# Two transformer layers on one core: bias and mask matmuls as pairs of 64-row tiles

## The chip, the cores and the metric

One core of a Trainium2 chip. The metric is the device time of one execution in microseconds (us). The kernel before took 1443.73 us (median of 3 runs, 1442.54 to 1447.4).

## What is computed

The input is 2 sequences of 1024 tokens with 128 channels. Two layers follow each other, each of the form x + attention(norm(x)) * silu(ffn(norm(x))). Only attention matters here:

```python
# layer 0: 16 heads of 8 channels, 2 x 1024 tokens, additive position bias, no mask
energy = jnp.einsum('bhqd,bhkd->bhqk', q, k)
rel = jnp.clip(pos[:, None] - pos[None, :] + (N - 1), 0, bias_table.shape[0] - 1)   # 249 rows
energy = energy + bias_table[rel].transpose(2, 0, 1)[None]
att = jax.nn.softmax(energy / (scaling * temp), axis=-1)
out = jnp.einsum('bhqk,bhkd->bhqd', att, v)
# layer 1: 16 heads of 8 channels, one sequence per batch, causal
attn = jnp.where(causal, jnp.einsum('bhqd,bhkd->bhqk', Q, K) * scale, -inf)
y = jnp.einsum('bhqk,bhkd->bhqd', jax.nn.softmax(attn, axis=-1), V)
```

The feed-forward parts are experts: ten in layer 0, a soft routed attention and eight experts in layer 1. As `rel` is clipped to 249 rows and N - 1 is 1023, the bias differs from a constant only where the key stands more than 775 positions after the query: queries of the first two tiles of 128, keys of the last two. The kernel subtracts the constant, which softmax does not see.

## The kernel before

Attention (`attention(l)` in each engine's block) works on groups G of four heads (j = 0 to 3), 8 groups in all, and on two halves of 512 queries in each: 16 halves H. Queries and keys are split in three bf16 parts and stacked on 48 rows (51 in the transposed form, where the maxima come in as three more rows). Heads j = 0 and 2 lie on partitions from 0, j = 1 and 3 on partitions from 64, so that their matmuls stand in different row halves of the array.

Each half has two kinds of scores:
- `s_unit`, 128 queries x up to 512 keys, in four PSUM banks used in turn (`RING`). DVE takes the row maximum of each (L1086), which frees the bank (`ring_free`). From the maxima POOL makes three bf16 parts (L670 to L673), PE turns them (unit "M"), and a DMA puts them as rows into the stack of queries.
- `st_step`, the transposed scores, 128 keys x up to 512 queries, with the maximum already subtracted, in three banks. ACT takes the exponential (L783), and `av_step` multiplies it with the values, four heads in four column tiles of 32.

Where the bias is not constant, or the causal diagonal lies, further matmuls add it into the same bank. In `s_unit` of layer 0, for key half 1 and query tiles 0 (256 columns) and 1 (128 columns), these are three full-array matmuls, one per bf16 part of the bias, with a flipped identity as weights. In `st_step` they are three for key tile 6 and six for key tile 7, with the bias tile `Hst` as weights and the flipped identity as moving operand. The bias tile is Toeplitz: DMAs read it from a DRAM row with a step of one element per partition (`load_bias`, L471). In layer 1, `mask` adds the causal mask as two matmuls of 64 rows in the head's own row half, each with 128 columns:

```python
for n, (w_, m_) in enumerate(zip(weights, moving)):
    ins = mm(out_, w_[row:row + 64, :], m_[row:row + 64, :], start=False, stop=n == 1)
```

`identb_sw` and `mask_kq_sw` are the same tables with their halves of 64 rows exchanged.

The order of PE's work is written out: `s_plan` deals the score units of the coming half over the steps of the present one, and the main loop issues, for each head j of a step, `st_step`, after j = 2 the `av_step` of the step before, and then the units dealt to it. All matmuls go through the helper `mm` (L1303). SP's queue carries all DMAs in program order: before layer 0 the split queries and keys, the bias rows (L531), the gate weights (L533, L541), and in the attention the stacks, bias tiles, maxima rows and the sums' way through DRAM.

The program gives each matmul a division of the array, as rows x columns of a tile: 64x128 for the scores, the transposed scores and the masks, 128x128 for the flips, 128x32 for the values, 128x64 for unit "M".

## Time and profile before

| | |
|---|---|
| median of 3 runs | 1443.73 us |
| profiled execution | 1445.76 us |
| its span | 1443.9 us |
| mean granted clock of TensorE | 0.845 of full speed |
| PE busy | 1172.7 us (81%) |
| DVE, ACT, POOL busy | 925.2, 699.2, 198.6 us |

Layer 0's attention runs from about 250 to 678 us, its transposed scores from 296 us; layer 1's from about 751 to 1121 us, its transposed scores from 810 us. In the rows, `PS<-arena 48*128 48x512` is a score matmul (weights of 48 rows by 128 columns, moving operand 48x512), `51*128` a transposed one, `128*32` a value matmul. The moving operand is named first: `PS<-flip,arena` is a bias matmul of the transposed scores, `PS<-arena,flip` one of the scores, `PS<-mask_kq,identb` a mask matmul of the transposed scores, `PS<-identb,mask_kq` one of the scores. A row of the timeline holds successive instructions with the same names; its length runs from the first start to the last end, and a matmul's end lies some 0.17 us behind its last column, so the distance of starts tells the pace. f32 matmuls appear as two records.

### The profile page before, as it was taken

What the parts mean: (1) busy time and instruction counts of PE and PEld (TensorE: products, weight loads), DVE (VectorE), ACT (ScalarE), POOL (GpSimd) and SP (SyncE); (2) the same over time, 40 slices, a digit from 0 to 9 for tenths busy, and PEclk for the clock granted to TensorE, in tenths of its full rate; (3) what the DMA queues carried; (4) which work ended last, traced back from release to release, by engine and by line L of the source; (5) the groups of instructions that cost most, each with busy time, mean ns of one, the idle gap of its engine ahead of it and who ended that gap; (6) DMA issues with size and microseconds to landing.
All of it is one profiled execution on the core that took longest, in us unless ns stands there. A gap on an engine that the chain in (4) does not pass through costs nothing.

```text
span 1443.9 us, 19168 instructions
## 1 busy us (share of the span) xinstructions
PE 1172.7 (81%) x6931; PEld 555.0 (38%) x6931; DVE 925.2 (64%) x1669; ACT 699.2 (48%) x1326; POOL 198.6 (14%) x292
## 2 busy tenths in 40 slices
PE   5599999779999999989741599889887597887477
PEld 3466666122232222221420244333331274464255
DVE  6687776859888988850651466666661145644577
ACT  5345444057777777774420166655664122121456
POOL 2155553000101100000000001111100300000200
PEclk9799999569999999995955588888885698898778
DMA  5512231501110011000455000000001500000050
GB/s 153 186 41 81 80 99 31 124 11 32 38 34 27 26 31 39 9 17 9 129 138 156 27 10 18 17 18 17 17 18 49 209 1 0 0 0 0 0 235 29
DMA packets 60995, 77.90 MB, mean 54 GB/s; under 512 B 15616, under 2 KB 39792, under 8 KB 57840
## 3 DMA queue, kind: packets, MB, share of 16 engines
q1 hardware_dynamic: 60912, 76.81, 17.2%
q8 instruction: 50, 0.82, 0.2%
q14 instruction: 33, 0.27, 0.1%
HBM read 61.58 MB, written 14.56 MB: 53 GB/s over the span
## 4 chain that ended last, share of the span: by engine, by line
PE 57%; DVE 17%; issue 7%; DMA 6%; ACT 6%; SPq 6%; POOL 1%; DVEq 0%; ACTq 0%; POOLq 0%
PE PS L1303 55%; DVE mx L1086 4%; SPq L464 3%; ACT arena L783 3%; DVE g_hi_lo L1176 3%; DMA arena<-sum_dram 2%; DMA arena<-mrow 2%; ACT g_hi_lo L834 1%; SPq L482 1%; DVE w_hi_lo L1279 1%; PE PS L1316 1%; SPq L449 1%; DVE arena L1288 1%; DMA k_dram<-arena 1%; DVE fw L1189 1%
## 5 line engine op out<-in xcount | busy, mean ns | idle before, releaser
L1303 PE MATMUL PS<-arena 128*32 128x512 f32 (+12 forms) x3680 | 665.1, 517 | 107.8 <-DMA arena<-mrow 78.8
L1086 DVE TENSOR_REDUCE mx<-PS 128x1 f32<-128x512 f32 (+3 forms) x896 | 509.6, 626 | 192.2 <-PE PS L1303 189.0
L783 ACT ACTIVATE arena<-PS 128x512 f32<-128x512 f32 (+3 forms) x896 | 440.9, 555 | 340.2 <-PE PS L1303 336.5
L1303 PEld LDWEIGHTS PS<-arena 128*32 128x32 f32 (+3 forms) x3680 | 168.4, 108 | 503.8 <-DVE mx L1086 138.9
L1176 DVE TENSOR_TENSOR g_hi_lo<-fw,g_hi_lo 128x512 fp32r<-128x512 f32 x80 | 91.7, 1147 | 48.2 <-ACT g_hi_lo L834 48.0
L1303 PE MATMUL PS<-x_hi,w_hi_lo 128*128 128x512 f32 x320 | 113.8, 398 | 0.9 <-DVE fw L1189 0.6
L712 POOL TENSOR_TENSOR fw<-fw,arena 128x512 f32<-128x512 f32 x64 | 90.8, 1423 | 101.0 <-DVE fw L1189 101.0
L842 ACT ACTIVATE fw<-PS 128x512 f32<-128x512 f32 x80 | 47.9, 599 | 97.8 <-PE PS L1303 97.8
L1303 PE MATMUL PS<-g_hi_lo,w_hi_lo 128*128 128x512 f32 x240 | 75.5, 424 | 15.7 <-DVE g_hi_lo L1176 15.7
L1303 PE MATMUL PS<-e_hi_lo,w_hi_lo 128*128 128x512 f32 x192 | 61.8, 404 | 11.7 <-DVE e_hi_lo L1232 11.7
L1303 PEld LDWEIGHTS PS<-x_hi,w_hi_lo 128*128 128x128 f32 x320 | 61.1, 191 | 17.7 <-issue 1.1
L1303 PE MATMUL PS<-x_lo,w_hi_lo 128*128 128x512 f32 x160 | 63.7, 398 | 0.0
L1303 PE MATMUL PS<-identb_sw,mask_kq_sw 64*128 64x128 bf16 x256 | 58.9, 244 | 0.0
L1303 PEld LDWEIGHTS PS<-g_hi_lo,w_hi_lo 128*128 128x128 f32 x240 | 39.7, 188 | 46.9 <-DVE g_hi_lo L1176 42.0
L1303 PE MATMUL PS<-identb,mask_kq 64*128 64x128 bf16 x256 | 57.5, 244 | 0.0
L1189 DVE TENSOR_TENSOR fw<-PS,fw 128x512 f32<-128x512 f32 x80 | 54.4, 680 | 4.7 <-ACT fw L842 4.7
L679 POOL TENSOR_TENSOR arena<-arena 128x512 f32<-128x512 f32 x16 | 20.3, 1271 | 262.4 <-DMA arena<-sum_dram 262.4
L1303 PE MATMUL PS<-mask_kq_sw,identb_sw 64*128 64x128 bf16 x256 | 52.9, 224 | 0.0
L1303 PE MATMUL PS<-mask_kq,identb 64*128 64x128 bf16 x256 | 52.5, 224 | 0.0
L1303 PE MATMUL PS<-e_hi_lo,fw_lo 128*128 128x512 f32 (+1 forms) x128 | 52.1, 407 | 0.0
L670 POOL CAST mparts<-mneg 128x16 bf16<-128x16 f32 x24 | 4.7, 198 | 340.0 <-DVE mneg L1079 340.0
L1316 PE MATMUL PS<-ident,arena 128*128 128x128 f32 x96 | 22.3, 405 | 35.6 <-DVE arena L974 27.9
(219 smaller groups left out, 1208.8 us busy)
## 6 DMA issues: line engine op xcount, KB each, us to landing
arena<-comb_dram SPq DMA_DIRECT2D x24, 1024.0 KB, 7.7
arena<-k_dram SPq DMA_DIRECT2D x16, 408.0 KB
q_dram<-arena SPq DMA_DIRECT2D x24, 256.0 KB, 3.7
k_dram<-arena SPq DMA_DIRECT2D x24, 256.0 KB, 3.8
arena<-q_dram SPq DMA_DIRECT2D x16, 384.0 KB
arena<-drev_dram SPq DMA_DIRECT2D x32, 192.0 KB, 3.6
fw<-sum_dram SPq DMA_DIRECT2D x16, 256.0 KB
arena<-sum_dram SPq DMA_DIRECT2D x16, 256.0 KB
```

The costliest lines, as they stand in the source:

```text
L449: sp.dma_start(dst, src).then_inc(qk_stored[l][b], 16)
L464: sp.dma_start(dst, src).then_inc(att[l][f"ld{n}"], 16)
L482: sp.dma_start(dst, mrow[first:first + 12, H % 2, :]).then_inc(A["m_ld"], 16)
L679: g.tensor_tensor(OT[:, G, 512 * h:512 * (h + 1)], Osb[:, h, :], RB[l][:, h, :], ALU.mult).then_inc(A["r_done"], 1)
L712: g.tensor_tensor(g_, g_, cwb[:, slot, 512 * (u // 2):512 * (u // 2 + 1)], ALU.mult).then_inc(gw_made, 1)
L783: s.activation(Pr[:, m % 8, 0:w], bank(4 + m % 3, 0, w), ACT.Exp).then_inc(A["e_done"], 1)
L842: s.activation(fa[:, u % 2, :], bank(2 * (u % 2)), ACT.Silu).then_inc(a_made, 1)
L1086: v.reduce_max(mx[:, H % 2, kh, n:n + 1], bank(U % RING, 0, w), axis=AX.X, negate=True).then_inc(A["ring_free"], 1)
L1176: v.tensor_tensor(g_r[1][:, u % 4, :], fg[:, u % 4, :], g_r[0][:, u % 4, :], ALU.subtract).then_inc(glo_made, 1)
L1189: v.tensor_tensor(fg[:, u % 4, :], bank(2 * (u % 2) + 1), fa[:, u % 2, :], ALU.mult).then_inc(g_made, 1)
L1303: return nc.tensor.matmul(out_, lhsT, rhs, start=start, stop=stop)
L1316: ins = nc.tensor.transpose(bank(first + c, P * k, P * (k + 1)), src(4 * c + k), ident[:, :])
```

## The change

The full-array bias matmuls are replaced by pairs of 64-row matmuls in the row half of the head, as the masks are, and each of these covers only 64 of the 128 queries. The bias tile in SBUF now holds, for each head, 64 partitions with both halves' values (`Hst[row:row+64, parity, pair, PARTS * half + part, :]`), which needs a second copy of the bias rows in DRAM, shifted by 64 (12 stores instead of 6), and `flip_sw`, the flipped identity with exchanged halves. Two helpers write the matmuls. `add_columns` (the bias of `st_step`, the masks of `s_unit`) restricts the moving operand to 64 columns. `add_rows` (the bias of `s_unit`, the masks of `st_step`) restricts the weights to 64 columns, so that the output has 64 partitions, except for the closing matmul of the bank, which has all 128. A matmul with 64 weight columns gets the division 64x64, one with 128 the division 64x128.

```diff
-        drev_dram = dram("drev_dram", (GROUPS, HG, PARTS, DREV), BF16)
+        drev_dram = dram("drev_dram", (GROUPS, HG, 2, PARTS, DREV), BF16)
...
-        Hst = bf(132, 12).rearrange("p (s j a c) -> p s j a c", s=2, j=HG, a=PARTS)
+        Hst = bf(132, 12).rearrange("p (s r x c) -> p s r x c", s=2, r=PAIRS, x=2 * PARTS)
...
                 for j in range(HG):
-                    src = bass.AP(tensor=drev_dram.tensor, offset=G * (HG * PARTS * DREV) + j * PARTS * DREV,
-                                  ap=[[1, P], [DREV, PARTS], [1, 256]])
-                    sp.dma_start(Hst[:, parity, j, :, :], src).then_inc(h_ld[parity], 16)
+                    row = 64 * (j % 2)
+                    src = bass.AP(tensor=drev_dram.tensor, offset=(G * HG + j) * 2 * PARTS * DREV,
+                                  ap=[[1, 64], [DREV, 2 * PARTS], [1, 256]])
+                    sp.dma_start(Hst[row:row + 64, parity, j // 2, :, :], src).then_inc(h_ld[parity], 16)
...
                 for b in range(BATCH):
-                    dst = drev_dram[b * NG:(b + 1) * NG, :, part, :].rearrange("g j n -> (g j) n")
-                    sp.dma_start(dst, dpart[:, part, :]).then_inc(drev_stored, 16)
+                    for half in range(2):
+                        dst = drev_dram[b * NG:(b + 1) * NG, :, half, part, 0:DREV - 64 * half].rearrange("g j n -> (g j) n")
+                        sp.dma_start(dst, dpart[:, part, 64 * half:DREV]).then_inc(drev_stored, 16)
...
+                    (flip_sw, [[1, P]], -(P // 2 - 1), 1, ALU.not_equal, 1.0),
...
+                    (flip_sw[:, :], [[1, P]], -(P + P // 2 - 1), 1, ALU.not_equal, 1.0),
...
-                def mask(out_, row, weights, moving):
-
-                    for n, (w_, m_) in enumerate(zip(weights, moving)):
-                        ins = mm(out_, w_[row:row + 64, :], m_[row:row + 64, :], start=False, stop=n == 1)
+                def half_rows(row, natural, swapped):
+
+                    return [(natural, swapped)[(half + row // 64) % 2][row:row + 64, :] for half in range(2)]
+
+                def add_rows(out_, permutation, first, moving, last):
+
+
+                    for half in range(2):
+                        ends = last and half == 1
+                        rows = slice(0, P) if ends else slice(first[half], first[half] + 64)
+                        ins = mm(out_[rows], permutation[half][:, rows], moving[half], start=False, stop=ends)
                     return ins
+
+                def add_columns(out_, weights, permutation, first, last):
+
+                    for half in range(2):
+                        c0 = first[half]
+                        ins = mm(out_[:, c0:c0 + 64], weights[half], permutation[half][:, c0:c0 + 64], start=False, stop=last and half == 1)
+                    return ins
+
+                FLIPPED, STRAIGHT = (64, 0), (0, 64)
...
                         for part in range(PARTS):
-                            ins = mm(bank(U % RING, h0, 512), flip[:, :], Hst[:, G % 2, j, part, 0:512 - h0], start=False, stop=part == PARTS - 1)
+                            rows = [Hst[row:row + 64, G % 2, pr, PARTS * half + part, 0:512 - h0] for half in range(2)]
+                            ins = add_rows(bank(U % RING, h0, 512), half_rows(row, flip, flip_sw), FLIPPED, rows, part == PARTS - 1)
                     if masked:
-                        order = (identb, identb_sw) if row == 0 else (identb_sw, identb)
-                        masks = (mask_kq, mask_kq_sw) if row == 0 else (mask_kq_sw, mask_kq)
-                        ins = mask(bank(U % RING, w - P, w), row, masks, order)
+                        ins = add_columns(bank(U % RING, w - P, w), half_rows(row, mask_kq, mask_kq_sw),
+                                          half_rows(row, identb, identb_sw), STRAIGHT, True)
...
-                    for n, (c0, lhsT) in enumerate(extra):
-                        ins = mm(bank(b_, c0, c0 + P), lhsT, flip[:, :], start=False, stop=n == len(extra) - 1)
+                    for n, (c0, part, x0) in enumerate(extra):
+                        weights = [Hst[row:row + 64, G % 2, pr, PARTS * half + part, x0:x0 + P] for half in range(2)]
+                        ins = add_columns(bank(b_, c0, c0 + P), weights, half_rows(row, flip, flip_sw), FLIPPED, n == len(extra) - 1)
                     if masked:
-                        order = (identb, identb_sw) if row == 0 else (identb_sw, identb)
-                        masks = (mask_kq, mask_kq_sw) if row == 0 else (mask_kq_sw, mask_kq)
-                        ins = mask(bank(b_, 0, P), row, order, masks)
+                        ins = add_rows(bank(b_, 0, P), half_rows(row, identb, identb_sw), STRAIGHT,
+                                       half_rows(row, mask_kq, mask_kq_sw), True)
```

The order of PE's instructions at three places. A row names output and inputs (the moving operand first) and the shape of the output, partitions x columns, and the semaphores it waits for. First, the transposed scores of key tile 6 in layer 0, before:

```order
L1303 MATMUL PS<-arena 128x512 [waits e_done0]
L1303 MATMUL PS<-flip,arena 128x128 x3
L1303 MATMUL PS<-arena 128x512 [waits ring_free0]
```

and now:

```order
L1308 MATMUL PS<-arena 128x512 [waits e_done0]
L1308 MATMUL PS<-flip,arena 128x64
L1308 MATMUL PS<-flip_sw,arena 128x64
L1308 MATMUL PS<-flip,arena 128x64
L1308 MATMUL PS<-flip_sw,arena 128x64
L1308 MATMUL PS<-flip,arena 128x64
L1308 MATMUL PS<-flip_sw,arena 128x64
L1308 MATMUL PS<-arena 128x512 [waits ring_free0]
```

Each matmul of 128 columns has become two of 64, all on 128 partitions. Second, the scores of query tile 0 in layer 0, before:

```order
L1303 MATMUL PS<-arena 128x512 [waits ring_free0,h_ld0]
L1303 MATMUL PS<-arena,flip 128x256 x3
L1303 MATMUL PS<-arena 128x512 [waits e_done0]
```

and now:

```order
L1308 MATMUL PS<-arena 128x512 [waits ring_free0,h_ld0]
L1308 MATMUL PS<-arena,flip 64x256
L1308 MATMUL PS<-arena,flip_sw 64x256
L1308 MATMUL PS<-arena,flip 64x256
L1308 MATMUL PS<-arena,flip_sw 64x256
L1308 MATMUL PS<-arena,flip 64x256
L1308 MATMUL PS<-arena,flip_sw 128x256
L1308 MATMUL PS<-arena 128x512 [waits e_done0]
```

Five write 64 partitions, the closing one 128. Third, masked scores and transposed scores in layer 1, before:

```order
L1303 MATMUL PS<-arena 128x384 [waits ring_free1]
L1303 MATMUL PS<-identb_sw,mask_kq_sw 128x128
L1303 MATMUL PS<-identb,mask_kq 128x128
L1303 MATMUL PS<-arena 128x384 [waits e_done1]
L1303 MATMUL PS<-mask_kq,identb 128x128
L1303 MATMUL PS<-mask_kq_sw,identb_sw 128x128
L1303 MATMUL PS<-arena 32x512 [waits e_done1]
```

and now:

```order
L1308 MATMUL PS<-arena 128x384 [waits ring_free1]
L1308 MATMUL PS<-identb_sw,mask_kq_sw 128x64
L1308 MATMUL PS<-identb,mask_kq 128x64
L1308 MATMUL PS<-arena 128x384 [waits e_done1]
L1308 MATMUL PS<-mask_kq,identb 64x128
L1308 MATMUL PS<-mask_kq_sw,identb_sw 128x128
L1308 MATMUL PS<-arena 32x512 [waits e_done1]
```

The scores' masks have half the columns, the transposed scores' first mask half the partitions, and the waits stand where they stood.

## Rows read from the trace of the kernel before

**Rows 1.** The page's chain of work that ended last, by line.
```profile
PE PS L1303 55%; DVE mx L1086 4%; SPq L464 3%; ACT arena L783 3%; DVE g_hi_lo L1176 3%; DMA arena<-sum_dram 2%; DMA arena<-mrow 2%; ACT g_hi_lo L834 1%; SPq L482 1%; DVE w_hi_lo L1279 1%; PE PS L1316 1%; SPq L449 1%; DVE arena L1288 1%; DMA k_dram<-arena 1%; DVE fw L1189 1%
```
**Rows 2.** Stretches: us; PE, PEld, DVE, ACT, POOL busy; clock, DMA share, GB/s.
```profile
296.00:635.00 339.00, 330.63 (x2300) 94.06 (x2296) 292.16 (x501) 256.03 (x485) 30.69 (x75) 0.98 0.10 26
405.64:428.56 22.92, 22.92 (x173) 7.52 (x173) 18.39 (x31) 15.65 (x30) 2.08 (x5) 1.00 0.17 48
810.00:1110.00 300.00, 264.62 (x2448) 113.72 (x2448) 190.70 (x423) 171.28 (x390) 33.40 (x81) 0.80 0.05 16
948.90:976.10 27.20, 26.38 (x283) 12.36 (x283) 20.28 (x43) 17.77 (x42) 2.45 (x6) 0.92 0.05 12
```
**Rows 3.** PE's instructions by form, 948.9 to 976.1 us: busy us, mean ns, idle before.
```profile
L1303 PE MATMUL PS<-mask_kq_sw,identb_sw 64*128 64x128 bf16 x32 | 6.4, 215 | 0.0
...
L1303 PE MATMUL PS<-identb_sw,mask_kq_sw 64*128 64x128 bf16 x28 | 5.7, 219 | 0.0
```
**Rows 4.** Timeline of PE, layer 0: start us, length us, instruction, count.
```profile
408.24 0.34 PE L1303 MATMUL PS<-flip,arena 128*128 128x128 bf16 x3
408.51 0.39 PE L1303 MATMUL PS<-arena 48*128 48x512 bf16 x2
408.83 0.34 PE L1303 MATMUL PS<-flip,arena 128*128 128x128 bf16 x3
409.11 1.39 PE L1303 MATMUL PS<-arena 128*32 128x512 f32 x10
...
411.46 0.39 PE L1303 MATMUL PS<-arena 48*128 48x512 bf16 x2
...
412.23 0.39 PE L1303 MATMUL PS<-arena 48*128 48x512 bf16 x2
```
**Rows 5.** Timeline of PE between the layers; the granted clock there is 0.50.
```profile
740.40 1.96 PE L1303 MATMUL PS<-n1T,router 128*32 128x512 f32 x8 [2.90 <-ACT arena L879]
742.08 1.99 PE L1303 MATMUL PS<-arena,sum_col 128*32 128x512 f32 x8
744.00 0.60 PE L1303 MATMUL PS<-simsq,ones 128*128 128x8 f32 x2
```
**Rows 6.** Timeline of PE in layer 1's routed attention.
```profile
1210.28 0.22 PE L1303 MATMUL PS<-mask_qk,identb 128*128 128x128 bf16 x1
1210.33 0.50 PE L1581 MATMUL PS<-ident,arena 128*128 128x128 f32 x3
```
**Rows 7.** Timeline of PE, layer 1 attention, masks.
```profile
858.76 0.22 PE L1303 MATMUL PS<-mask_kq,identb 64*128 64x128 bf16 x1
858.82 0.21 PE L1303 MATMUL PS<-mask_kq_sw,identb_sw 64*128 64x128 bf16 x1
...
863.03 0.22 PE L1303 MATMUL PS<-identb,mask_kq 64*128 64x128 bf16 x1
...
863.87 0.21 PE L1303 MATMUL PS<-identb_sw,mask_kq_sw 64*128 64x128 bf16 x1
```
**Rows 8.** Groups of instructions, one group of heads of layer 0, 405.64 to 451.47 us.
```profile
L1086 DVE TENSOR_REDUCE mx<-PS 128x1 f32<-128x512 f32 x65 | 40.7, 683 | 5.1 <-PE PS L1303 4.7
```
**Rows 9.** Timeline of PE, layer 0, scores with bias.
```profile
418.54 0.39 PE L1303 MATMUL PS<-arena 48*128 48x512 bf16 x1
...
419.30 0.39 PE L1303 MATMUL PS<-arena 51*128 51x512 bf16 x2
...
424.79 0.39 PE L1303 MATMUL PS<-arena 51*128 51x512 bf16 x2
...
425.38 0.39 PE L1303 MATMUL PS<-arena 51*128 51x512 bf16 x2
```
**Rows 10.** Who waited for whom, 948.9 to 976.1 us: us, times, longest.
```profile
PEld PS L1303 <- DVE mx L1086: 6.8, 10, 1.7
...
PEld PS L1303 <- ACT arena L783: 3.3, 9, 0.6
```
**Rows 11.** Timeline of SP's queue before layer 0's experts.
```profile
44.70 3.43 SPq L531 DMA_DIRECT2D drev_dram<-arena  x6
```

More of the change, by code:

```diff
@@ L202, in block_net @@
         flip = sb("flip", [P, P], BF16)
+        flip_sw = sb("flip_sw", [P, P], BF16)
         identb_sw = sb("identb_sw", [P, P], BF16)
@@ L562, in _ @@
             load_stacks(0, 2)
-            sp.wait_ge(drev_stored, 16 * PARTS * BATCH)
+            sp.wait_ge(drev_stored, 16 * PARTS * BATCH * 2)
             sp.wait_ge(y_done, 8 * FFN_SEQ)
@@ L623, in _ @@
             g.memset(sum_col[:, EXP:EXP + 1], 1.0)
-            for t_ in (ident, identb, flip, mask_kq, mask_qk, identb_sw, mask_kq_sw):
+            for t_ in (ident, identb, flip, flip_sw, mask_kq, mask_qk, identb_sw, mask_kq_sw):
                 g.memset(t_[:, :], 0.0)
@@ L1191, in ffn_units @@
                         weights_lo(n + 1, 1 - slot)
-            dve.wait_ge(drev_stored, 16 * PARTS * BATCH)
+            dve.wait_ge(drev_stored, 16 * PARTS * BATCH * 2)
             ffn_experts(dve, ffn_units)
@@ L1424, in st_step @@
                     if l == 0 and h == 0 and kt == KT - 2:
-                        extra = [(0, Hst[:, G % 2, j, part, 0:P]) for part in range(PARTS)]
+                        extra = [(0, part, 0) for part in range(PARTS)]
                     if l == 0 and h == 0 and kt == KT - 1:
-                        extra = [(q * P, Hst[:, G % 2, j, part, P * (1 - q):P * (2 - q)]) for q in range(2) for part in range(PARTS)]
+                        extra = [(q * P, part, P * (1 - q)) for q in range(2) for part in range(PARTS)]
                     masked = l == 1 and kt * P == q0
```

## The prediction

> **What bounds the kernel now.** I read the page's chain first, then the busy time by stage, then the forms of TensorE's instructions, and last its timeline around the matmuls that the diff touches. The chain lies on PE for 57% of the span, and 55% is line L1303, the matmul helper [rows 1]. By stage [rows 2]: in layer 0's attention (296 to 635 us) PE is busy 330.6 of 339 us at a clock of 0.98, in layer 1's (810 to 1110 us) 264.6 of 300 at 0.80. A group of four heads takes 45.8 us in layer 0. Its first half, which holds the bias matmuls, keeps PE busy throughout (22.92 us; DVE 18.4), so there every nanosecond of PE counts. In layer 1 a group takes some 36.5 us. In 27.2 of them, from 948.9 us, PE is busy 26.4 us at a clock of 0.92, and in the rest the sums go through DRAM and PE waits. The masks stand nearly all in the 27.2 us: the transposed scores' in two forms of 32 matmuls, the scores' in two of 28, one of each shown [rows 3]. So PE's time counts in layer 0's first halves and in layer 1's 27 us.
>
> **What a change of the array's division costs.** Every matmul names a tile of the array, and the timeline shows what it costs to pass from one division to another. Layer 0 [rows 4]: a pair of 512-column matmuls in the two row halves starts at 408.51 us, the full-array flips at 408.83. 512 columns at 2.4 GHz are 0.213 us, so 0.105 us are lost. Three flips cover 0.34 us and one 0.22, so they stand 0.06 us apart (56 ns is what such rows give on longer runs, and 128 columns at 2.4 GHz are 53), but the next matmul comes 0.27 us after the first flip, not 0.17: another 0.095 us. **The rows also show a change of columns alone**: flips on 128x128, then values on 128x32, all with 128 rows, 408.83 to 409.11: 0.28 us, the same 0.1 us too much. At 1.2 GHz the same [rows 5]: eight matmuls on 128x32 take 1.68 us before the next eight start (740.40 to 742.08), and the 128x128 matmul after these comes 1.92 us on, 0.2 too late. It isn't the type: after 128 columns of bf16 an f32 matmul on the same division starts 0.05 us on, 1210.28 to 1210.33 [rows 6]. So I take 0.1 us for each change of division at 2.4 GHz, rows or columns.
> The Trainium skill, TensorEngine Tiling (Array Packing), Tiling Modes, says that changing the mode, not just the tile, drains the engine. It gives no price. It lists 64x64 and 64x128 as two modes, and for that pair no row here shows the price.
>
> **Layer 0, transposed scores (st_step).** 288 full-array flips (by the loops of st_step: 32 places with 3 and 32 with 6) become 576 of 64 columns in the head's own 64 rows with all 128 output partitions: the division of the scores themselves. Both changes of division go. A place with 3 takes 0.59 us now (408.24 to 408.83), one with 6 0.77 (411.46 to 412.23). After: 0.213 us plus 6 or 12 short matmuls. Their spacing s isn't in the trace: 64 columns at 2.4 GHz are 27 ns, the lower end; 56 ns, the flips' own spacing, is the upper, if the weight load or the issue binds. The densest stretch of layer 1 starts 22 matmuls from 863.03 to 863.87, 40 ns apart with their weights and with longer matmuls among them [rows 7]: I take 38 ns. Then 0.44 and 0.67 us, 32 x (0.15 + 0.10) = 8.0 us less; but 16 of the places stand before a value step, whose own change stays: 16 x 0.095 = 1.5 less. **Minus 6.5 us** (27 ns: minus 12.8; 56 ns: plus 3.9). DVE leaves room for it: 40.7 us of reductions in 45.8 [rows 8].
>
> **Layer 0, scores (s_unit).** 192 flips on the full array become 384: of each six, five make 64 partitions (division 64x64) and the last all 128. Two changes before, two after. Today 0.76 us with 256 columns (418.54 to 419.30) and 0.59 with 128 (424.79 to 425.38) [rows 9]. After: 0.213, 0.105, then three rounds if the two column halves of one row half run side by side, as the four value matmuls on 128x32 do, 0.095, and the last matmul, which the next one in the other row half may cover. 256 columns: 0.213 + 0.105 + 3 x 0.107 + 0.095 = 0.73 to 0.84; 128: 0.57 to 0.62. With the middles 32 x 0.025 + 32 x 0.01, **plus 1 us**; at most plus 10 if the halves do not run side by side (32 x 0.32 more).
>
> **Layer 1, transposed scores: the largest term.** 256 masked scores are closed by two mask matmuls of 128 columns, both on 64x128. The two start 0.06 us apart, 858.76 and 858.82 [rows 7]. After, the first mask makes 64 partitions on 64x64, the second all 128 on 64x128. Columns and matmuls stay the same, and two changes of division come in, which were not there: 0.105 + 0.095 = **0.2 us** each. A drain also stops the other row half, which today streams meanwhile (up to 0.1 more), and at 1.2 GHz it costs some 0.2 instead of 0.1 [rows 5]. In a group's 27.2 us stand 32 such scores: 6.4 us. What absorbs it: in these 27.2 us the weight loader waits 6.8 us for DVE's reductions and 3.3 for ACT's exponentials [rows 10], but PE idles only 0.8 us, as most of these waits lie under streaming matmuls. I let 1.5 us be absorbed (0.8 to 5).
>
> **Layer 1, scores.** 512 masks of 128 columns become 512 of 64 columns on the same division, 56 ns to s: 28 units x 2 x 18 ns = 1.0 us per group (0 to 1.6). Together 6.4 - 1.5 - 1.0 = 3.9 us a group, eight groups, **plus 31 us** (0 to 70).
>
> **Small parts.** Bias tiles: the same four issues a group, half the partitions and twice the rows of 512 bytes; they run two groups ahead, except the first, which shares SP's queue with the stacks before layer 0. There PE also runs six flips for three, at the lower clock, before the first maxima go out; I add 0.5 us (minus 1 to plus 2). SP issues six more stores of the bias rows, and six take 3.43 us [rows 11]. Behind them stands the store of the gate weights, whose load only the second expert needs: the first expert's matmuls hide it, and without them it would be at most the 3.4 us. The same stores hold DVE, which waits for ACT there anyway. POOL makes one memset and two selects more before const_done, which let the first transposes start later; the layer norm on DVE, which the next ones need, is the longer way. I cost both at nothing.
>
> **Sum.** The profiled execution took 1445.8 us: 1445.8 - 6.5 + 1.0 + 0.5 + 31 = 1471.8. It stands 2.0 above the median 1443.7, so **1470 us**.
> A second rule against the change: the Trainium skill, TensorE: Matmul & The Clock Gate, Part 2 (Weight-path perf modes), gives the fast weight load to weights of 128 columns only. The new weights on 64x64 have 64. By its formula (columns over 1.2 per ns) such a load is 53 ns, an estimate. Exposed behind a drain 256 times that adds some 10 us to the sum. No row here has 64 columns of weights.
>
> **Rivals.**
> 1. *Only a change of rows drains.* Then 64x64 beside 64x128 is free. For it: no row has that pair. Against it: the change from 128x128 to 128x32 costs what the others cost [rows 4, 5]. The scores' bias becomes 0.213 + 4 x 0.107 less half a round, 0.59 for 0.76, and 0.40 for 0.59: 32 x 0.36 = minus 11.5. With minus 6.5 and, in layer 1, minus 6 (1.0 a group, three quarters felt): minus 24, **1420 us**, faster. It decides from 0.05 us per change downwards: there layer 1's cost is 1.6 us a group and is absorbed. The skill's rule on modes (same page as above) speaks against this rival. Chance 0.18.
> 2. *The changes cost, and are absorbed*: layer 1 takes up 5 us of the 6.4 a group, as DVE and ACT catch up while PE drains. The chain has only some 4 us of DVE and ACT in the stretch. 6.4 - 5 - 1.0 = 0.4, times eight plus 3, layer 0 minus 5: **1442 us**. Chance 0.09.
> 3. *Worse than counted*: 0.3 us a masked score since the other half stops too, s = 56 ns, and the lower clock in more of layer 1. (9.6 - 1.5) x 8 + 3.9 + 1.5 = plus 70, **1514 us**. Chance 0.13.
> The change may also do less than its name says: the closing matmul of each group is not a 64-row by 64-partition tile but the full width. That is in the terms above.
>
> **Numbers.** Forecast as worked out (1450 to 1490): 0.60. Some 0.3% (4.3 us) is what a measurement of this kernel can tell from none. Faster by more than that: rival 1 and a little of rival 2, 0.20; within: 0.06; slower: 0.74. The range 1425 to 1500 leaves out most of rival 1 (about 0.11) and the upper part of rival 3 (0.08).
>
> **What would show it.** In layer 1 the second mask of a transposed score should start 0.15 us after the first (0.06 now) and the first 0.1 later than its score's columns allow; the 27.2 us stretch should be near 31. In layer 0 six 64-column flips should fit in 0.23 us and a place with 3 take 0.44 us; a scores' bias with 256 columns 0.73 to 0.84. If a 64x64 matmul follows one on 64x128 without the 0.1 us, rival 1 holds and the forecast is wrong in sign. If PE's spacings are as I say and the group still takes 37 us, it is rival 2.

## The result and the profile after

The changed kernel takes 1483.53 us in the median of 4 runs (1476.8 to 1491.6), against 1445.57 us of the kernel before on the same chip in 4 runs: a ratio of 1.0267, 95% interval 1.0209 to 1.0325. In a later set of runs it took 1487.38 us beside 1444.44, ratio 1.0316 (1.0282 to 1.035). It is slower. The forecast was 1470 us, so the sign is right, the value lies in the range, and the cost is nearly half as large again as forecast (38 us for 26).

The first line is the chain by line of the changed kernel, to be read against [rows 1]: the matmul helper (now L1308) has 58% of the span instead of 55%.

```profile
PE PS L1308 58%; SPq L465 3%; DVE g_hi_lo L1181 3%; DMA arena<-sum_dram 2%; DVE mx L1091 2%; ACT arena L788 2%; DMA arena<-mrow 1%; ACT g_hi_lo L839 1%; SPq L484 1%; DVE w_hi_lo L1284 1%; SPq L450 1%; DVE arena L1293 1%; DMA sum_dram<-rsums 1%; DMA k_dram<-arena 1%; PE PS L1321 1%
```

Next come the stretches of the kernel before, cut at the instructions that bound the stages: from the first transposed score of layer 0 to the output projection, the same of layer 1, inside the latter one group of heads (from the second unit "M" of one group to that of the next), and the six inner groups together. Columns as in [rows 2].

```profile
295.82:679.92 384.10, 368.71 (x2469) 101.06 (x2470) 294.96 (x507) 278.98 (x527) 34.02 (x81) 0.94 0.09 25
810.26:1119.33 309.07, 273.43 (x2509) 116.76 (x2509) 190.99 (x424) 174.59 (x400) 33.40 (x81) 0.79 0.06 20
948.90:985.40 36.50, 33.58 (x323) 14.54 (x323) 24.32 (x53) 21.97 (x50) 4.50 (x11) 0.83 0.06 17
837.70:1059.10 221.40, 197.84 (x1935) 87.73 (x1933) 147.20 (x319) 131.65 (x300) 26.99 (x66) 0.83 0.06 17
```

The same of the changed kernel, with a second group of layer 1 at a lower clock:

```profile
301.62:667.10 365.48, 348.20 (x2925) 104.97 (x2925) 293.81 (x507) 275.80 (x527) 33.88 (x81) 0.97 0.10 26
...
794.98:1157.99 363.01, 336.20 (x2508) 129.49 (x2509) 195.98 (x424) 183.45 (x400) 33.52 (x81) 0.74 0.06 19
957.50:998.90 41.40, 39.21 (x323) 15.78 (x323) 25.05 (x53) 22.96 (x50) 4.54 (x11) 0.83 0.05 15
998.90:1049.30 50.40, 47.48 (x323) 17.85 (x323) 25.29 (x53) 23.18 (x50) 4.54 (x11) 0.64 0.04 12
825.80:1091.30 265.50, 244.43 (x1934) 97.40 (x1932) 150.70 (x319) 137.88 (x300) 27.22 (x66) 0.78 0.05 14
```

Layer 0's attention is 18.6 us shorter and layer 1's 53.9 us longer. The first transposed score of layer 0 starts 5.8 us later, and the stretches between and behind the two attentions are 2.5 and 2.9 us shorter, which nearly cancels. Of the 18.6 us only 8.6 belong to the eight groups of heads (44.75 us each for 45.83); 9.8 lie behind the last unit "M" (26.85 us for 36.62), where the granted clock differs from run to run (see the last section).

In the group of layer 1 shown, the same 323 matmuls keep PE busy for 39.21 us instead of 33.58 at the same mean clock of 0.83. Its idle time differs from group to group, so the six inner groups together are the better measure: PE idles 21.1 us of them for 23.6 before, that is 3.5 us a group for 3.9. There was almost nothing to absorb the new time. In the second profile of the changed kernel layer 0 takes 372.1 us and layer 1 356.7, and PE idles 3.8 us a group.

What a masked transposed score costs now is to be seen in the timeline of the changed kernel in layer 1, at full clock, against 0.06 us between two masks in [rows 7].

```profile
967.74 0.38 PE L1308 MATMUL PS<-arena 51*128 51x512 bf16 x1
968.05 0.24 PE L1308 MATMUL PS<-mask_kq_sw,identb_sw 64*64 64x128 bf16 x1
968.22 0.23 PE L1308 MATMUL PS<-mask_kq,identb 64*128 64x128 bf16 x1
968.22 0.33 PE L1308 MATMUL PS<-arena 48*128 48x384 bf16 x1
```

A score of 512 columns (0.213 us) holds the 64x64 mask back for 0.31 us, the closing 64x128 mask comes 0.17 us later, and the next matmul, in the other row half, starts with it. Over all such places of the profile at full clock the medians are 307 ns where 213 would do, 173 instead of 59, then 4 instead of 55 in the other row half, or 156 instead of 144 before a value step.

In layer 0 the transposed scores' bias, against [rows 4], and the scores' bias, against [rows 9] (a "place" is one bank with its bias matmuls):

```profile
413.62 0.39 PE L1308 MATMUL PS<-arena 51*128 51x512 bf16 x1
...
413.70 0.38 PE L1308 MATMUL PS<-arena 48*128 48x512 bf16 x1
413.85 0.19 PE L1308 MATMUL PS<-flip,arena 64*128 64x64 bf16 x1
413.88 0.19 PE L1308 MATMUL PS<-flip_sw,arena 64*128 64x64 bf16 x1
...
414.12 0.39 PE L1308 MATMUL PS<-arena 51*128 51x512 bf16 x1
...
420.32 0.29 PE L1308 MATMUL PS<-arena,flip_sw 64*64 64x256 bf16 x1
420.33 0.29 PE L1308 MATMUL PS<-arena,flip 64*64 64x256 bf16 x1
...
420.57 0.27 PE L1308 MATMUL PS<-arena,flip_sw 64*64 64x256 bf16 x1
420.77 0.28 PE L1308 MATMUL PS<-arena,flip 64*128 64x256 bf16 x1
...
421.09 0.29 PE L1308 MATMUL PS<-arena,flip 64*64 64x256 bf16 x1
```

The 64-column matmuls stand 0.03 us apart, and the score of the other row half (413.70) runs under them: from one transposed score with six parts to the next it is 0.50 us (413.62 to 414.12), where [rows 4] had 0.77 (411.46 to 412.23). In the scores' bias the two column halves do run side by side (420.32 and 420.33), then come 0.2 us before the closing matmul, and one place with 256 columns takes 0.77 us (420.32 to 421.09), as long as the one in [rows 9] (0.76).

### The profile page after: what moved, and what is told of

It reads as the page before. It is cut to its first block, busy times and chain, and to the rows that moved or that the text cites. A ratio compares the mean times of both kernels' runs of the same rounds, so it can differ in the third digit from the quotient of the medians.

```text
span 1479.7 us, 20139 instructions
## 1 busy us (share of the span) xinstructions
PE 1208.4 (82%) x7411; PEld 568.3 (38%) x7411; DVE 928.3 (63%) x1669; ACT 704.5 (48%) x1326; POOL 199.1 (13%) x295
## 4 chain that ended last, share of the span: by engine, by line
PE 59%; DVE 15%; issue 7%; DMA 7%; SPq 6%; ACT 5%; POOL 1%; DVEq 0%; ACTq 0%; POOLq 0%
PE PS L1308 58%; SPq L465 3%; DVE g_hi_lo L1181 3%; DMA arena<-sum_dram 2%; DVE mx L1091 2%; ACT arena L788 2%; DMA arena<-mrow 1%; ACT g_hi_lo L839 1%; SPq L484 1%; DVE w_hi_lo L1284 1%; SPq L450 1%; DVE arena L1293 1%; DMA sum_dram<-rsums 1%; DMA k_dram<-arena 1%; PE PS L1321 1%
## 5 line engine op out<-in xcount | busy, mean ns | idle before, releaser
L1308 PE MATMUL PS<-arena 128*32 128x512 f32 (+12 forms) x3680 | 688.2, 518 | 99.8 <-DMA arena<-mrow 75.3
L788 ACT ACTIVATE arena<-PS 128x512 f32<-128x512 f32 (+3 forms) x896 | 447.1, 556 | 376.6 <-PE PS L1308 369.1
L1308 PEld LDWEIGHTS PS<-arena 128*32 128x32 f32 (+3 forms) x3680 | 173.7, 109 | 462.5 <-DVE mx L1091 130.4
L1308 PE MATMUL PS<-x_hi,w_hi_lo 128*128 128x512 f32 x320 | 113.6, 397 | 1.3 <-DVE fw L1194 1.0
L1308 PE MATMUL PS<-g_hi_lo,w_hi_lo 128*128 128x512 f32 x240 | 75.4, 423 | 15.8 <-DVE g_hi_lo L1181 15.8
L1308 PE MATMUL PS<-e_hi_lo,w_hi_lo 128*128 128x512 f32 x192 | 62.5, 408 | 12.0 <-DVE e_hi_lo L1237 12.0
L1308 PEld LDWEIGHTS PS<-x_hi,w_hi_lo 128*128 128x128 f32 x320 | 61.0, 190 | 17.8 <-issue 1.4
L1308 PE MATMUL PS<-x_lo,w_hi_lo 128*128 128x512 f32 x160 | 63.4, 396 | 0.0
L1308 PE MATMUL PS<-mask_kq,identb 64*64 64x128 bf16 (+1 forms) x256 | 62.7, 248 | 0.0
L1308 PE MATMUL PS<-mask_kq_sw,identb_sw 64*128 64x128 bf16 (+1 forms) x256 | 62.4, 248 | 0.0
L1308 PEld LDWEIGHTS PS<-g_hi_lo,w_hi_lo 128*128 128x128 f32 x240 | 39.6, 188 | 47.1 <-DVE g_hi_lo L1181 42.7
L1308 PE MATMUL PS<-e_hi_lo,fw_lo 128*128 128x512 f32 (+1 forms) x128 | 52.7, 412 | 0.0
L1321 PE MATMUL PS<-ident,arena 128*128 128x128 f32 x96 | 21.1, 389 | 36.3 <-DVE arena L979 28.0
L839 ACT ACTIVATE g_hi_lo<-fw 128x512 fp32r<-128x512 f32 x80 | 49.8, 624 | 0.8 <-DVE fw L1194 0.8
L1308 PE MATMUL PS<-identb,mask_kq 64*128 64x64 bf16 x256 | 48.5, 216 | 0.0
```

Of the source, the lines that this page charges most:

```text
L788: s.activation(Pr[:, m % 8, 0:w], bank(4 + m % 3, 0, w), ACT.Exp).then_inc(A["e_done"], 1)
L839: s.activation(g_r[0][:, u % 4, :], fg[:, u % 4, :], ACT.Copy).then_inc(ghi_made, 1)
L1308: return nc.tensor.matmul(out_, lhsT, rhs, start=start, stop=stop)
L1321: ins = nc.tensor.transpose(bank(first + c, P * k, P * (k + 1)), src(4 * c + k), ident[:, :])
```

## The experiments

There were nine runs, in three sets: e1 to e4, then e5, e6, e7 and the changed kernel again, then e8. The kernel before took 1444.07, 1444.44 and 1442.68 us beside them, and each ratio is to the kernel before of the same set.

**e1: the masks of the transposed scores as before, all else as changed.**

```diff
                     if masked:
-                        ins = add_rows(bank(b_, 0, P), half_rows(row, identb, identb_sw), STRAIGHT,
-                                       half_rows(row, mask_kq, mask_kq_sw), True)
+                        for half in range(2):
+                            ins = mm(bank(b_, 0, P), half_rows(row, identb, identb_sw)[half],
+                                     half_rows(row, mask_kq, mask_kq_sw)[half], start=False, stop=half == 1)
```

> The changed kernel, but the masks of the transposed scores in layer 1 as they were: both matmuls make all 128 partitions, so no 64x64 beside 64x128 is left there. Theory (the two changes of division per masked transposed score are the loss): the group of layer 1 falls from 42 to 50 us in the changed kernel to 36 to 37, first mask to second from 173 ns to about 60, and the time to 1430 to 1443 us, ratio to before 0.990 to 0.998: layer 0's groups keep their 1.1 us each, against 5.8 us more before the first transposed scores. Rival (the loss is the lower clock, the scores' masks or the bias part): it stays above 1465 us, ratio above 1.013.

Measured: 1432.68 us (1424.44 to 1433.59, 6 runs), ratio 0.9915 (0.9888 to 0.9942), as the theory had it. One edit of the change costs 51 us; without it the change is a gain of 0.85%. Layer 1's attention takes 308.1 us again, and its inner groups 36.5 us in the mean (before 36.9).

**e2: only the masks of the transposed scores as changed, all else as before.** In the kernel before:

```diff
-                        ins = mask(bank(b_, 0, P), row, order, masks)
+                        mm(bank(b_, 0, P)[0:64], order[0][row:row + 64, 0:64], masks[0][row:row + 64, :], start=False, stop=False)
+                        ins = mm(bank(b_, 0, P), order[1][row:row + 64, :], masks[1][row:row + 64, :], start=False)
```

> The kernel before, with this one part of the change: the first mask matmul of each transposed score in layer 1 makes 64 partitions, the second 128. Theory: the whole loss of layer 1 and none of layer 0's gain: the group of layer 1 takes 42 to 45 us, the time is 1488 to 1505 us, ratio 1.03 to 1.04. Rival: below 1465 us.

Measured: 1496.29 us (1487.2 to 1500.78, 4 runs), ratio 1.0352 (1.0312 to 1.0392), as the theory had it. Layer 0 is as before, layer 1 takes 362.8 us. The six inner groups together:

```profile
842.00:1099.70 257.70, 225.65 (x1933) 94.02 (x1932) 150.12 (x319) 137.80 (x300) 27.32 (x66) 0.90 0.05 15
```

An inner group takes 42.95 us in the mean, 6.1 more than before. PE is busy 4.6 us of these longer, at a higher clock (0.90 for 0.83), and idles 1.4 us longer (32.1 us in the six groups for 23.6): nothing is absorbed. The two halves of the change multiply to the whole: 0.9915 x 1.0352 = 1.0264, for 1.0267 measured.

**e3: as e1, with the scores' masks of layer 1 as before too, so that only the biases are new.**

```diff
-                        ins = add_columns(bank(U % RING, w - P, w), half_rows(row, mask_kq, mask_kq_sw),
-                                          half_rows(row, identb, identb_sw), STRAIGHT, True)
+                        for half in range(2):
+                            ins = mm(bank(U % RING, w - P, w), half_rows(row, mask_kq, mask_kq_sw)[half],
+                                     half_rows(row, identb, identb_sw)[half], start=False, stop=half == 1)
```

> As e1_tmasks_back, with the scores' masks of 128 columns again, so only the bias part of the change is left. It prices the halved columns of the scores' masks: at 28 ns for 64 columns (measured in layer 0 of the changed kernel) against 56, 32 units of two masks a group would give 1.8 us a group if all were on the path; I expect 0 to 8 us above e1_tmasks_back, 1434 to 1450 us. If the masks' columns count in full it is 10 us or more.

Measured: 1434.48 us (1432.04 to 1440.07, 7 runs), ratio 0.9937 (0.9916 to 0.9957). Against e1 the halved masks of the scores are worth 1.8 us, less than the spread of either kernel, where the forecast took 8. The profiles say a little more: an inner group takes 37.3 us in the profile of e3 (its longest run), 36.9 in that of the kernel before, whose instructions in layer 1 are the same, and 36.5 in those of e1 and e4.

**e4: as e1, with the scores' bias on all 128 output partitions (64x128) instead of 64x64.**

```diff
-                        rows = slice(0, P) if ends else slice(first[half], first[half] + 64)
+                        rows = slice(0, P)
```

> As e1_tmasks_back, with the scores' bias in layer 0 on all 128 output partitions too: six matmuls on 64x128, no 64x64 left in the kernel. A place with 256 columns is then 0.213 + 6 x 0.107 = 0.855 us, with 128 columns 0.213 + 6 x 0.055 = 0.54, both less what the other row half runs beside them; now they take about 0.75 to 0.86 and 0.6. Theory (division changes cost 0.1 us each): the two nearly cancel, group of layer 0 44.2 to 45.4 us, time within 6 us of e1_tmasks_back. If 64x64 were cheap to enter, it would be slower by 4 x (0.32 + 0.16) us a group, 15 us in all.

Measured: 1424.74 us (1423.02 to 1428.54, 4 runs), ratio 0.9877 (0.9848 to 0.9906). That is 7.9 us under e1, where I had expected at most 6. A group of layer 0 takes 43.19 us; I had expected 44.2 to 45.4, and so undervalued what 64x64 costs in layer 0. The timeline shows why: the matmuls are 0.11 us apart, but no time is lost between two of them, and scores of the other row half stream under them.

```profile
408.11 0.27 PE L1308 MATMUL PS<-arena,flip_sw 64*128 64x256 bf16 x1
408.12 0.39 PE L1308 MATMUL PS<-arena 48*128 48x512 bf16 x1
408.22 0.27 PE L1308 MATMUL PS<-arena,flip 64*128 64x256 bf16 x1
408.33 0.27 PE L1308 MATMUL PS<-arena,flip_sw 64*128 64x256 bf16 x1
...
408.69 0.39 PE L1308 MATMUL PS<-arena 48*128 48x512 bf16 x1
```

From score to score it is 0.57 us (408.12 to 408.69), against 0.77 in the changed kernel and 0.76 in that before.

**e8: as e1, with the scores' bias on the full array**, to split layer 0's gain.

```diff
                         for part in range(PARTS):
-                            rows = [Hst[row:row + 64, G % 2, pr, PARTS * half + part, 0:512 - h0] for half in range(2)]
-                            ins = add_rows(bank(U % RING, h0, 512), half_rows(row, flip, flip_sw), FLIPPED, rows, part == PARTS - 1)
+                            ins = mm(bank(U % RING, h0, 512), flip[:, :], Hst[:, G % 2, pr, PARTS * (j % 2) + part, 0:512 - h0], start=False, stop=part == PARTS - 1)
```

> How layer 0's gain divides between the two kinds of bias. It is e1_tmasks_back with the scores' bias as three full-array matmuls again, as in the kernel before; as the bias tile has the new layout, these read 128 partitions that belong to two heads, so the values added to the scores of layer 0 are not the reference's, while forms, counts and durations are those of before. Only the transposed scores' bias is then new in layer 0. Before: a group of layer 0 takes 45.83 us; with both changes 44.76; with the scores' bias on 64x128 43.19. From the spacing of the new 64-column matmuls, 28 ns, a place with three parts takes 0.213 + 6 x 0.028 = 0.38 us for 0.59 and one with six 0.55 for 0.77; 8 places, and in two of four the change of division stays: 8 x 0.215 - 2 x 0.095 = 1.5 us less. Theory: 44.2 to 44.5 us a group; then the scores' bias as changed costs 0.3 to 0.5 us a group instead of the 0.13 forecast, and on 64x128 it gains some 1.2. Rival, the forecast's own split (38 ns): 45.0 us, and the scores' bias as changed would gain 0.25. Whole time 1430 to 1437 us.

Measured: 1435.11 us (1417.54 to 1438.42, 10 runs), ratio 0.9935 (0.9904 to 0.9965). A group of layer 0 takes 44.45 us, for 45.83 before, 44.76 as changed and 43.19 in e4. So the transposed scores' bias gains 1.38 us a group (11 us in all), the scores' bias as changed gives back 0.31 (2.5 us), and on 64x128 it gains 1.26 (10 us, and e4's time is 10.4 us under e8's). The 2.5 us rest on the groups alone: by the whole times e8 is not faster than e1, but 2.4 us slower, in another set and with spreads of 21 and 9 us. The full-array form, for the comparison with e4:

```profile
411.93 0.50 PE L1308 MATMUL PS<-arena,flip 128*128 128x256 bf16 x3
412.37 0.39 PE L1308 MATMUL PS<-arena 48*128 48x512 bf16 x1
412.69 0.50 PE L1308 MATMUL PS<-arena,flip 128*128 128x256 bf16 x3
```

**e6: as e4, with 96 weight columns in the first mask of the transposed scores.** The division stays 64x128, but the weights are narrower than 128.

```diff
+                            keys = slice(0, 96 if half == 0 else P)
-                            ins = mm(bank(b_, 0, P), half_rows(row, identb, identb_sw)[half],
+                            ins = mm(bank(b_, 0, P)[keys], half_rows(row, identb, identb_sw)[half][:, keys],
                                      half_rows(row, mask_kq, mask_kq_sw)[half], start=False, stop=half == 1)
```

> Which property of the first mask matmul costs the time in layer 1: the division 64x64, or weights narrower than 128 columns? It is e4_no_64x64 with the first mask matmul of each transposed score on 96 weight columns (96 output partitions), which still gets the division 64x128. Theory (the change of division costs): nothing happens, the second mask starts 0.06 us after the first, a group of layer 1 takes 36 to 37 us, time 1422 to 1428, as e4. Rival (narrow weights load slowly and the load is exposed): the second mask starts 0.1 us or more after the first, a group of layer 1 takes 38 to 42 us, time 1440 to 1475. Between them, if narrow weights account for the 20 ns by which the second mask in the changed kernel was later than two changes of division explain: 0.08 us, and at most 5 us in all.

Measured: 1422.44 us (1421.32 to 1424.46, 4 runs), ratio 0.9845 (0.982 to 0.9871), the same as e4.

```profile
896.74 0.38 PE L1308 MATMUL PS<-arena 51*128 51x512 bf16 x1
896.96 0.22 PE L1308 MATMUL PS<-mask_kq,identb 64*96 64x128 bf16 x1
897.02 0.21 PE L1308 MATMUL PS<-mask_kq_sw,identb_sw 64*128 64x128 bf16 x1
897.16 1.33 PE L1308 MATMUL PS<-arena 128*32 128x512 f32 x9
```

0.22, 0.06 and 0.14 us, as with full weights. Yet the loads themselves are longer. PE's weight loads by form, layer 1's attention, with count, busy us and mean ns:

```profile
L1308 PEld LDWEIGHTS PS<-mask_kq,identb 64*96 64x96 bf16 x127 | 16.8, 132 | 1.1 <-issue 0.3
...
L1308 PEld LDWEIGHTS PS<-mask_kq,identb 64*128 64x128 bf16 x127 | 12.8, 101 | 3.0 <-issue 0.2
```

132 ns for 96 columns and 101 for 128, and the 31 ns more lie under streaming matmuls. Weights of 96 columns by themselves cost no time here; the division does.

**e7: as e4, with both masks of the transposed scores on 64x64**, in the two column halves.

```diff
+                            keys = slice(64 * half, 64 * half + 64)
-                            ins = mm(bank(b_, 0, P), half_rows(row, identb, identb_sw)[half],
-                                     half_rows(row, mask_kq, mask_kq_sw)[half], start=False, stop=half == 1)
+                            ins = mm(bank(b_, 0, P)[keys], half_rows(row, identb, identb_sw)[half][:, keys],
+                                     half_rows(row, mask_kq, mask_kq_sw)[half], start=False, stop=True)
```

> Both mask matmuls of a transposed score in layer 1 on 64x64, one in each column half of the head's row half, the rest as e4_no_64x64. The number of changes of division around a masked score is the same as in the changed kernel (one in, one out), but none stands between the two masks. Theory (each change costs about 0.1 us, and two column halves of one row half run side by side): the first mask still starts 0.3 us after a 512-column score, the second 0.02 to 0.06 us after the first, the next matmul 0.15 us after that. A group of layer 1 takes 39.5 to 42 us, 1 to 2 less than in the changed kernel and 3 to 6 more than e4; time 1450 to 1470. Rival (narrow weights cost, not the change): there are now twice as many of them, and it is slower than e4 plus the changed kernel's 50 us: over 1475. Second rival (the cost lies only in going from 64x64 to 64x128 while that row half's partial tile still runs): then under 1440.

Measured: 1497.38 us (1493.72 to 1497.83, 4 runs), ratio 1.036 (1.0331 to 1.0388). Each step is as the theory had it, at full clock (first) and at half (second):

```profile
872.50 0.38 PE L1308 MATMUL PS<-arena 51*128 51x512 bf16 x1
872.80 0.24 PE L1308 MATMUL PS<-mask_kq_sw,identb_sw 64*64 64x128 bf16 x1
872.80 0.24 PE L1308 MATMUL PS<-mask_kq,identb 64*64 64x128 bf16 x1
872.98 0.33 PE L1308 MATMUL PS<-arena 48*128 48x384 bf16 x1
...
882.64 0.61 PE L1308 MATMUL PS<-arena 51*128 51x512 bf16 x1
883.18 0.31 PE L1308 MATMUL PS<-mask_kq,identb 64*64 64x128 bf16 x1
883.19 0.31 PE L1308 MATMUL PS<-mask_kq_sw,identb_sw 64*64 64x128 bf16 x1
883.43 1.20 PE L1308 MATMUL PS<-arena 128*32 128x128 f32 x10
```

The two masks start together, and the next matmul 0.17 us behind. But the time is far outside my 1450 to 1470, on the side of the rival whose mechanism these rows contradict. What I had left out is the granted clock. In one group, 868 to 916 us:

```profile
868.00:882.00 14.00, 14.00 (x121) 5.10 (x113) 7.73 (x15) 8.59 (x20) 1.27 (x1) 0.99 0.06 19
...
882.00:916.00 34.00, 30.96 (x207) 11.15 (x209) 17.85 (x40) 14.85 (x33) 3.27 (x10) 0.50 0.04 10
```

After 14 us in which PE was busy without a break, the clock stands at 1.2 GHz for 34 us. In the whole of layer 1 258 of the 512 mask matmuls of the transposed scores start at that level, against 116 and 100 in the two profiles of the changed kernel and 50 before; a group takes 47.1 us in the mean. Why the clock is lower for so much longer than in the changed kernel (0.78 over its inner groups) these runs don't tell. So e7 confirms the spacings, misses the time, and shows that the spacings alone don't give it.

**e5: as e4, with fewer moving columns.** The first mask of a transposed score covers 64 queries, and the scores' bias leaves out 64 keys for the second 64 queries.

```diff
                     for half in range(2):
                         ends = last and half == 1
                         rows = slice(0, P)
-                        ins = mm(out_[rows], permutation[half][:, rows], moving[half], start=False, stop=ends)
+                        c0 = 64 * (1 - half)
+                        ins = mm(out_[rows, c0:], permutation[half][:, rows], moving[half][:, c0:], start=False, stop=ends)
...
-                            ins = mm(bank(b_, 0, P), half_rows(row, identb, identb_sw)[half],
-                                     half_rows(row, mask_kq, mask_kq_sw)[half], start=False, stop=half == 1)
+                            c1 = 64 * (half + 1)
+                            ins = mm(bank(b_, 0, c1), half_rows(row, identb, identb_sw)[half],
+                                     half_rows(row, mask_kq, mask_kq_sw)[half][:, 0:c1], start=False, stop=half == 1)
```

> A version that may beat both kernels. It is e4_no_64x64 with fewer moving columns: the first mask matmul of a transposed score in layer 1 covers 64 queries instead of 128 (keys 0 to 63 are hidden only from queries 0 to 63), and of each pair of scores' bias matmuls the one for queries 64 to 127 leaves out 64 keys (192 for 256, 64 for 128). All of them stay on 64x128. Theory (columns cost PE time at 2.4 GHz, 64 columns 27 ns, and no division changes): layer 0 loses 3 x 27 ns in each of 8 places a group, 0.65 us a group, all of it felt: its group 42.6 us for e4's 43.2. Layer 1: 32 x 28 ns = 0.9 us a group, of which little to most is felt (halving the scores' masks was felt by about a sixth). Time 1417 us, range 1412 to 1421. Rival (the load of the weights or the issue binds at short matmuls, not the columns): a 64-column mask then stands no nearer to the next than a 128-column one, layer 1 stays, and the time is 1420 to 1424.

Measured: 1417.78 us (1401.92 to 1423.78, 6 runs), ratio 0.9776 (0.9733 to 0.9819, without the longest run): the fastest version, 1.8 to 2.7% under the kernel before.

```profile
894.52 0.38 PE L1308 MATMUL PS<-arena 51*128 51x512 bf16 x1
894.74 0.19 PE L1308 MATMUL PS<-mask_kq,identb 64*128 64x64 bf16 x1
894.77 0.21 PE L1308 MATMUL PS<-mask_kq_sw,identb_sw 64*128 64x128 bf16 x1
894.92 1.33 PE L1308 MATMUL PS<-arena 128*32 128x512 f32 x9
```

The 64-column mask is 0.03 us from the next, so at this size its columns bind and not the weight load. The total is as expected, its parts are not: a group of layer 0 gains 0.27 us instead of 0.65 (42.92 for 43.19), a group of layer 1 0.3 in the mean (36.1 for 36.5). Together that is some 5 us of the 7 by which the time is under e4's.

**The changed kernel again.**

> The changed kernel once more, on the chip and in the job of these experiments, to see what of its profile is lasting. The first transposed score of layer 0 started 5.8 us later in its profile than in that before; three experiments with the same bias rows and stores start it as before, so I expect 296 us here and not 301.6. The groups of layer 1 took 41.4 to 50.4 us; if the two long ones came from a lower granted clock at that moment, they stand elsewhere or not at all here, and layer 1 takes 345 to 363 us. Time 1470 to 1490.

Measured: 1487.38 us (1481.35 to 1495.62, 4 runs). The first transposed score of layer 0 starts at 296.5 us, so the 5.8 us of the first profile were not lasting. The long groups of layer 1 stand at other places than in the first profile or are shorter (46.2 and 46.5 us, the others 41.4 to 41.9):

```profile
960.80:1002.20 41.40, 36.42 (x322) 15.20 (x322) 24.95 (x53) 22.88 (x50) 4.55 (x11) 0.91 0.05 15
1002.20:1048.70 46.50, 43.15 (x322) 16.59 (x322) 24.90 (x53) 22.98 (x50) 4.54 (x11) 0.72 0.04 13
```

Two groups with the same instructions, 5.1 us apart, the longer with the lower clock. The clock isn't all, though: the first of these and the group of the first profile shown above both take 41.4 us, at 0.91 and at 0.83. PE is busy 36.4 us in one and 39.2 in the other and idles the rest.

## Why the prediction was right in sign and low in size

**The cost of a change of division** held: 0.1 us for 64x128 to 64x64, columns alone, in one row half. Measured are 0.094 us going in (307 - 213) and 0.117 coming out (173 in e7 where a 128-column matmul needs 56). Rival 1, that only a change of rows drains, is refuted by these spacings and by the time of e2. The Trainium skill, TensorEngine Tiling (Array Packing), Tiling Modes, has the rule that a change of mode drains; for this pair of modes the traces now agree and give the price. The Trainium skill, TensorE: Matmul & The Clock Gate, Part 2 (Weight-path perf modes), gives the fast weight load to weights of 128 columns only. The traces agree that narrower weights load longer (132 ns for 101 in e6), but the time did not feel it: the change to 64x64 costs 0.094 us with the narrow load behind it, no more than the 0.105 that the prediction read at a change with full weights. The 10 us that the prediction named for it beside the sum (256 x 53 ns would be 13.6) did not come.

**Layer 1, the transposed scores' masks**: forecast 6.4 us a group less 1.5 absorbed, 4.9; measured 6.1 in e2. By the spacings at full clock it is 24 x (94 + 114 - 51) ns + 8 x (94 + 114 + 12) ns = 5.5 us, somewhat under my 6.4, since the next score in the other row half starts with the closing mask. The failed step is "I let 1.5 us be absorbed": PE's idle time in a group rose by 1.4 us in e2, and fell by only 0.4 and 0.1 in the two profiles of the changed kernel. I had read that PE idles only 0.8 us in the dense stretch, which was the better guide. Rival 2, absorption, is refuted with it. What exceeds the 5.5 in e2 is this longer idling; why PE idles longer there stays open. A lower clock can't be the reason, as e2's is higher than before (0.90 for 0.83).

**Layer 1, the scores' masks**: forecast minus 1.0 us a group. Without the division changes around them it is minus 0.2 by the times (e3 against e1) and minus 0.4 to 0.8 by the profiled groups (36.5 for 36.9 and 37.3). With them, the regular groups of the changed kernel (41.4 to 41.9 us, second profile) are 1 to 1.5 us shorter than e2's 42.95, but with the two long groups its mean is 43.2, and layer 1 takes 363.0 and 356.7 us for e2's 362.8. So the gain shows in the regular groups alone, and that the term holds where PE is the bound is likely and not shown.

**Layer 1's clock**: the sum had no term for it. At 41.6 us a regular group (second profile) against 36.9 the layer would lose 8 x 4.7 = 38 us; it lost 48 there and 54 in the first profile, and the long groups are where the rest is: in the second profile 46.2 and 46.5 us, both at 0.72 of full speed (9.5 more than regular ones), in the first 46.6 and 50.4 us, at 0.72 and 0.64. Rival 3 had the lower clock in it, at a chance of 0.13; its 1514 us were too much.

**Layer 0, the transposed scores' bias**: forecast minus 6.5, measured minus 11.0 us (8 x 1.38). The spacing s was 28 to 29 ns, not 38: my choice came from a row in which longer matmuls stood between, and the columns' own 27 ns was the right end. The full 12.8 of that end was not reached.

**Layer 0, the scores' bias**: forecast plus 1.0, measured plus 2.5 us; side by side, as assumed, with places of 0.77 us inside the 0.73 to 0.84 forecast.

**Small parts** at about nothing: held, as the start of layer 0's transposed scores in the second profile shows (0.7 us later). The 5.8 us of the first profile did not come again.

With the measured terms: 1445.8 - 11.0 + 2.5 + 38 = 1475, and 9.5 for the two long groups makes 1485; the second profile's execution took 1481.35. Of the difference 3.2 us lie at the start of layer 0's transposed scores: up to the second unit "M" they take 14.94 us at a clock of 0.79 (296.53 to 311.47 us), and 18.14 at 0.56 in the kernel before (295.82 to 313.96). The first profile of the changed kernel has 18.10 at 0.57, so this is the clock and not the edit. The forecast's errors in layer 0 (3 us too little gained) and in layer 1 (7 us too little lost with regular groups, and 10 to 16 more in the long ones) went opposite ways. That the value lies so near is partly luck: the long groups at a low clock, the largest single miss, have no term in the sum.

## What to carry to other kernels

Before narrowing a matmul to a quarter of the array, look at its neighbours' division: the narrow one saved nothing here while its moving columns stayed, and going in and out cost some 0.2 us, 256 times. Save moving columns instead, which paid here down to 64; keep the full output width, so that the other row half goes on. And where the diff mixes an edit of columns with one of output rows, cost and test them apart: here one gave 0.9% and the other took 3.5%. And read what PE can absorb from all groups of a stage, since the idle time of a single one ran from 2.9 to 4.7 us in the same kernel.

## What was unexpected

- Matmuls of 64 columns, each with its own weights, run 28 to 29 ns apart in long rows (12 of them in 0.35 us), so neither the weight load nor the issue binds at that size.
- Two matmuls on 64x64 in the two column halves of one row half start 3 ns apart.
- At 1.2 GHz this change of division is not twice as dear: 0.11 us in (534 to 536 ns in the median behind a 512-column score, which needs 427) and 0.14 us out (243 less 107). The prediction took 0.2 from [rows 5], for another pair of divisions.
- The granted clock differed with the form of the masks: in e7 it stood at 0.50 for 34 of 48 us of a group, with as many columns streamed as in the changed kernel. The cause is open; no run was made for it.
- The last 32 us of layer 0's attention ran at 0.50 in nine of the eleven profiles, that of the kernel before and the second of the changed kernel among them, and at 0.89 in the first of the changed kernel and in e1:

```profile
648.00:679.90 31.90, 29.34 (x104) 3.64 (x104) 0.25 (x1) 17.12 (x33) 1.27 (x1) 0.50 0.03 9
```

  That is the kernel before; and the changed one, first profile:

```profile
635.00:667.10 32.10, 23.47 (x189) 6.29 (x187) 2.09 (x5) 21.00 (x41) 3.32 (x6) 0.89 0.04 13
```

  From the last unit "M" on it is 36.62 us in one and 26.85 in the other. The clock at the start of the transposed scores varies too (14.9 to 18.2 us up to the second "M"), and the two profiles of the changed kernel, whose groups are all 44.75 us long, end with layer 0 attentions of 365.5 and 372.1 us. So the clock alone moves a run by some 7 us. The six runs of e1 stand at 1424 to 1426 us (two, one of them the profiled one with 0.89) and 1432 to 1434 us (four), which fits but was not traced. The runs of e5 and e8 spread by 22 and 21 us, which this does not explain.
